# Pre-LN decoder layer on one Trainium2 core: where the causal mask of the self layer's second half of heads is applied

## The reference, cut to what matters

```
x: (16, 128, 128)   16 images (batch entries) of 128 rows (positions) by 128 columns; 16 heads of 8 columns
def self_attention(x):                      # no weights: q = k = v = the heads of x
    w = einsum('bhqd,bhkd->bhqk', q, k) / sqrt(8)
    w = where(tril(ones(128, 128)), w, most_negative)
    return einsum('bhqk,bhkd->bhqd', softmax(w), v)
x = x + self_attention(layernorm(x))
x = x + cross_attention(layernorm(x), ctx, bias)     # projections, bias (16, 16, 128, 128), softmax
x = x + ffn_block(layernorm(x))                      # attention with weights, then 8 experts, one chosen for each row
```

## Time and profile before

| | |
|---|---|
| time, median of 3 runs | 429.36 us (429.25, 429.36, 431.63) |
| span of the profiled execution | 431.3 us |
| time of the profiled execution | not listed apart; 431.63, the slowest of the three, is the only one longer than the span, by 0.3 us |
| busy in the span | PE 313.1, PE weight load 203.1, DVE 249.6, ACT 198.4, POOL 254.1 us |
| self layer (slots 0 to 15) | about 16 to 105 us of the span |
| cross layer with its hand-over from the self layer | about 91 to 212 us |

### The profile page before, as it was taken

The page is one execution under the profiler, slowest core; times in us unless marked ns, Lnnn a source line. Parts: engine busy times, 40 slices in busy tenths (PEclk is TensorE's granted clock), DMA queues, the critical chain, the costliest instruction groups (busy, mean ns, idle before and its releaser), DMA issues.

```text
span 431.3 us, 9910 instructions
## 1 busy us (share of the span) xinstructions
PE 313.1 (73%) x3435; PEld 203.1 (47%) x3435; DVE 249.6 (58%) x592; ACT 198.4 (46%) x390; POOL 254.1 (59%) x365
## 2 busy tenths in 40 slices
PE   1376888776779999989778788898875500199994
PEld 0133333432456666666544444444443400099893
DVE  5135454458999999997356455665622250067773
ACT  3347555544455565565344536456464200045451
POOL 5853343315889898999996638736340327324454
PEclk9969888999999999999899989999997555589998
DMA  6101443210358977921125990000000002323330
GB/s 165 31 2 56 123 117 110 74 38 14 97 156 184 219 191 162 212 27 22 12 26 136 283 297 24 2 2 2 2 2 2 1 24 108 95 53 103 93 90 18
DMA packets 67040, 36.36 MB, mean 84 GB/s; under 512 B 36253, under 2 KB 56864, under 8 KB 66992
## 3 DMA queue, kind: packets, MB, share of 16 engines
q1 hardware_dynamic: 57040, 15.79, 17.4%
q10 hardware_dynamic: 8448, 16.78, 13.7%
q0 software_dynamic: 1504, 3.16, 2.1%
HBM read 28.48 MB, written 7.69 MB: 84 GB/s over the span
## 4 chain that ended last, share of the span: by engine, by line
PE 43%; issue 16%; POOL 15%; DVE 13%; ACT 8%; DVEq 1%; DMA 1%; POOLq 0%; ACTq 0%; SPq 0%
PE pair_banks L562 23%; PE work_bank L562 9%; POOL biased L413 4%; DVE biased L1019 4%; ACT xn L847 4%; POOL routed_rows L545 3%; PE pair_banks L565 3%; PE work_bank L565 3%; PE small_bank L565 3%; PE small_bank L562 2%; POOL rstd L380 2%; DVE rowmax L1034 1%; ACT outT L886 1%; DVE att L1065 1%; POOL q_lane L390 1%
## 5 line engine op out<-in xcount | busy, mean ns | idle before, releaser
L880 ACT ACTIVATE probs<-pair_banks 128x1024 f32<-128x1024 f32 x96 | 97.5, 1023 | 68.6 <-PE pair_banks L565 36.0
L413 POOL TENSOR_TENSOR biased<-biased,rowmax 128x1024 f32<-128x1024 f32 x32 | 60.5, 1899 | 15.7 <-DVE rowmax L1026 15.5
L562 PE MATMUL work_bank<-probs,vaug 128*32 128x128 f32 x1536 | 53.6, 282 | 5.5 <-ACT hn2T L894 3.4
L562 PEld LDWEIGHTS work_bank<-probs,vaug 128*32 128x32 f32 x1536 | 40.3, 112 | 15.7 <-issue 8.6
L1041 DVE TENSOR_TENSOR pair_banks<-pair_banks,causal 128x1024 f32<-128x1024 f32 x16 | 19.7, 1233 | 47.7 <-PE pair_banks L562 47.7
L1034 DVE TENSOR_REDUCE rowmax<-pair_banks 128x8 f32<-128x1024 f32 x32 | 38.9, 1215 | 13.5 <-PE pair_banks L562 13.5
L374 POOL TENSOR_SCALAR vareps<-meanvar 128x2 f32<-128x2 f32 x32 | 7.4, 233 | 62.6 <-DVE meanvar L995 61.5
L562 PE MATMUL pair_banks<-q_lane,kT 32*128 32x512 f32 x256 | 42.3, 734 | 1.7 <-DVE biased L1019 1.7
L1019 DVE TENSOR_TENSOR biased<-pair_banks,bias_in 128x1024 f32<-128x1024 f32 x32 | 38.8, 1214 | 7.3 <-PE pair_banks L562 3.8
L552 POOL DMA_INDIRECT out<-vaug x23 | 22.6, 984 | 33.1 <-DVE vaug L1230 20.3
L562 PE MATMUL pair_banks<-k_lane,qT 32*128 32x512 f32 x256 | 37.5, 654 | 5.9 <-DVE biased L1019 4.0
(11 more groups left out here) (143 smaller groups left out, 581.0 us busy)
## 6 DMA issues: line engine op xcount, KB each, us to landing
bias_in<-in_w SPq DMA_DIRECT2D x16, 256.0 KB, 7.3
routed_rows<-filler SPq DMA_DIRECT2D x2, 1028.0 KB, 9.1
vaug<-routed_rows SPq DMA_DIRECT2D x23, 64.5 KB
biased<-routed_rows SPq DMA_DIRECT2D x23, 64.0 KB
ctx_in<-in_ctx SPq DMA_DIRECT2D x8, 128.0 KB, 4.1
att_scratch<-att SPq DMA_DIRECT2D x16, 64.0 KB, 5.4
att_rows<-att_scratch SPq DMA_DIRECT2D x16, 64.0 KB, 2.9
routed_rows<-filler SPq DMA_DIRECT2D x1, 899.5 KB, 12.0
```

What stands on the lines that cost most here:

```text
L413: nc.gpsimd.tensor_tensor(v, v, rowmax[:, b % 2, 8 * half:8 * half + 8].unsqueeze(2).to_broadcast([128, 8, S]), ALU.subtract).then_inc(s_s ...
L562: return nc.tensor.matmul(o, lhsT, rhs, start=start, stop=stop, **kw)
L880: nc.scalar.activation(probs[:, b % 2, 2 * half:2 * half + 2, :], pair("exp", b, half), ACT.Exp, scale=1.0 if layer(b) == CROSS else SCALE ...
```

## The change

For heads 8 to 15 of the self layer the scores are exponentiated as they are; POOL then multiplies the two quarters `probs[:, b % 2, 2:4, :]` in place by `allowed`, a 128x128 tile of ones and zeros broadcast over the eight heads. `s_masked` now stands for that product, and `add_outputs(b)` waits for it. DVE's addition of the mask is gone, and `exponentials(b, 1)` waits for the scores alone. `allowed` is built by POOL at the start (a memset and a select), in the place of `zero`, which nothing used. The first half is masked as before.

```diff
--- before.py
+++ after.py
@@ -118,7 +118,7 @@
         identb = sb("identb", [128, 128], bf16)
         causal = sb("causal", [128, G, S], bf16)
         pick = sb("pick", [128, G, S], bf16)
-        zero = sb("zero", [128, 1])
+        allowed = sb("allowed", [128, S])
         minus_half = sb("minus_half", [128, 4])
         att_rows = sb("att_rows", [128, 2, D])
         wx = {k: sb("w_" + k, [128, D]) for k in ("xq", "xk", "xv", "xo", "fq", "fk", "fv", "fo")}
@@ -209,6 +209,7 @@
         s_maxT = sem("maxT_ready")
         s_e = sem("scores_ready")
         s_masked = sem("second_half_masked")
+        s_allowed = sem("allowed_ready")
         s_p = sem("probs_ready")
         s_pv = sem("outputs_added")
         s_out = sem("out_copied")
@@ -413,6 +414,13 @@
                 nc.gpsimd.tensor_tensor(v, v, rowmax[:, b % 2, 8 * half:8 * half + 8].unsqueeze(2).to_broadcast([128, 8, S]),
                                         ALU.subtract).then_inc(s_sub, 1)
 
+            def mask_probabilities(b):
+                pool.wait_ge(s_allowed, 2)
+                pool.wait_ge(s_p, 2 * b + 2)
+                v = probs[:, b % 2, 2:4, :].rearrange("p g (h k) -> p (g h) k", k=S)
+                nc.gpsimd.tensor_tensor(v, v, allowed[:].unsqueeze(1).to_broadcast([128, 2 * G, S]),
+                                        ALU.mult).then_inc(s_masked, 1)
+
             def max_parts(b):
                 i, n = b % 2, b - FIRST_FFN
                 pool.wait_ge(s_mfree, 2 * (b - B) + 2)
@@ -474,6 +482,10 @@
             nc.gpsimd.affine_select(out=causal[:], in_=causal[:], compare_op=ALU.is_ge, fill=MASKED, base=0,
                                     pattern=[[0, G], [1, S]], channel_multiplier=-1).then_inc(s_ident, 1)
             inverse_deviation(1)
+            nc.gpsimd.memset(allowed[:], 1.0).then_inc(s_allowed, 1)
+            pool.wait_ge(s_allowed, 1)
+            nc.gpsimd.affine_select(out=allowed[:], in_=allowed[:], compare_op=ALU.is_ge, fill=0.0, base=0,
+                                    pattern=[[1, S]], channel_multiplier=-1).then_inc(s_allowed, 1)
             pool.wait_ge(s_lane, 4)
             self_queries(0)
             pool.wait_ge(s_dve_const, 1)
@@ -512,6 +524,8 @@
                     inverse_deviation(3)
                 if b in LAST_NORMS:
                     inverse_deviation(NP + LAST_NORMS[b])
+                if 1 <= b <= FIRST_CROSS:
+                    mask_probabilities(b - 1)
                 if maxes:
                     subtract_maxes(b + 2, 0)
                 if b % 2 == 0 and CROSS_PAIR <= q + 2 < NP:
@@ -690,6 +704,7 @@
                 claim("work")
                 pe.wait_ge(s_p, 2 * b + 2)
                 if layer(b) == SELF:
+                    pe.wait_ge(s_masked, b + 1)
                     pe.wait_ge(s_vself, b // 2 + 1)
                 else:
                     pe.wait_ge(s_v, b // 2 - CROSS_PAIR + 1)
@@ -872,10 +887,7 @@
                 last.then_inc(s_qkT, 1)
 
             def exponentials(b, half):
-                if layer(b) == SELF and half == 1:
-                    act.wait_ge(s_masked, b + 1)
-                else:
-                    act.wait_ge(s_e, 2 * b + half + 1)
+                act.wait_ge(s_e, 2 * b + half + 1)
                 wait(act, s_pv, b - 1)
                 nc.scalar.activation(probs[:, b % 2, 2 * half:2 * half + 2, :], pair("exp", b, half), ACT.Exp,
                                      scale=1.0 if layer(b) == CROSS else SCALE).then_inc(s_p, 1)
@@ -1034,13 +1046,6 @@
                     nc.vector.tensor_reduce(peak, banks.rearrange("p g (h k) -> p (g h) k", k=S),
                                             AX.X, ALU.max).then_inc(s_mfree, 1)
 
-            def mask_second_half(b):
-                dve.wait_ge(s_ident, 5)
-                dve.wait_ge(s_e, 2 * b + 2)
-                banks = pair("exp", b, 1)
-                nc.vector.tensor_tensor(banks, banks, causal[:].rearrange("p g k -> p (g k)").unsqueeze(1).to_broadcast(
-                    [128, 2, G * S]), ALU.add).then_inc(s_masked, 1)
-
             def take_maxT(b):
                 dve.wait_ge(s_mtr, b - FIRST_FFN + 1)
                 if b - 2 >= FIRST_FFN:
@@ -1102,8 +1107,6 @@
                     norm_stats(NP + LAST_NORMS[b])
                 if maxes:
                     row_maxes(b + 2, 0, FIRST_STEP)
-                if b < FIRST_CROSS:
-                    mask_second_half(b)
                 if 0 <= b - 2 < NB:
                     attention(b - 2)
                 if b == 4:
```

## The result

| | before | changed |
|---|---|---|
| median | 429.31 us (428.9 to 431.63, 4 runs) | 438.92 us (438.42 to 439.2, 4 runs) |
| ratio | | 1.0184, 95% interval 1.0136 to 1.0232 |

The change makes the kernel slower by 1.8%. I had said 430.0 us, range 426.5 to 434.0, and 0.77 for a move within 1%: the time lies outside the range.

A forecast was written before the change was run, and what follows sets the result against it. A chain of waits was taken to bound the self layer. Terms 1.4 - 1.2 - 0.6 + 0.55 = +0.15 us, plus 0.5 for the clock, gave +0.65 on the median 429.36: 430.0 us, range 426.5 to 434.0.

The forecast's parts named there:

- What bounds the kernel, and the chain: Self layer: no engine full, a chain of waits across odd and even slots sets the pace, 9.98 us a pair.
- Even images free, odd ones not: Self layer: even images' products fit 4.5 us before PE wants them; odd images' stand behind the deviation and delay PE.
- The price of one product, 1.90 us: POOL: each of 16 products takes 1.90 us, like the subtraction in place, 30.4 us in all.
- The handover from POOL to PE, 0.05 us: Odd image's chain: 0.05 us between the end of POOL's product and PE's output product.
- the 0.69 that I had: Self layer: the odd image's chain takes 7.28 us against 6.59, so each pair comes 0.69 us later.
- The clock, "0.25 us off" a pair, and 0.5 us once: PE: slow stretch falling partly on a wait saves 0.25 us a pair; longer gaps add 0.5 us once.
- My lag of 1.4 us behind the four pairs: Slot 10: four pairs at 0.45 us each, less 0.4 gained in slot 2, leave 1.4 us of lag.
- Handed back in slots 11 to 13, 1.2 us, and in 14 and 15, 0.6: Slots 11 to 13 each gain about 0.4 us; slots 14 and 15 gain 0.6 from two masks off DVE.
- Hand-over, 0.55 us: Where the cross layer begins: image 14's product fits POOL's idle time, image 15's makes POOL 0.55 us late.
- POOL becomes the bound at the hand-over: Rival, chance 0.12: products of images 14 and 15 cost 1.90 us each in the row-maxima ring; +5.2, 434.6 us.
- The port, priced at 0: DVE's additions to x_sb beside POOL's products cost 0, other end 1.35 us a pair; rival 435.4 us, chance 0.06.
- The gain from removing DVE's mask, 0.37 us in each even slot: Even self slots: the second exponential starts at 50.37 in place of 50.74, gaining 0.37 us if nothing else waits.

The follow-up runs named there:

- e4: Changed kernel with POOL multiplying for images 0, 2, ... 12 only and DVE masking the others: 426.47 us, ratio 0.9882 to before.
- e10: Changed kernel with POOL multiplying for images 1, 3, ... 13 only and DVE masking the others: 437.78 us, ratio 1.0134 to before.
- e9: Changed kernel with seven idle matmuls ahead of PE's wait for each odd image's product (images 3 to 15): 434.60 us, ratio 1.0043 to before.
- e15: Kernel before with five idle matmuls in each even self slot, where PE waits for ACT: 426.37 us, ratio 0.9876 to before.
- e12: Changed kernel without the products of images 14 and 15, nothing in their place: 434.39 us, ratio 1.0057 to before.
- e5: Kernel before, DVE masks kept, with 16 added POOL products on a tile nobody reads and PE not waiting: 435.18 us, ratio 1.0107 to before.
- e8: Changed kernel with DVE's residual addition in the self layer replaced by a reduction with one SBUF input: 434.89 us, ratio 1.008 to before.
- e1: Changed kernel without POOL's product and PE's wait for it, so no mask on heads 8 to 15: 420.90 us, ratio 0.9723 to before.

## Why the prediction was wrong

- **What bounds the kernel, and the chain:** right. The chain through statistics, deviation and product exists as laid out; up to the end of POOL's shift I had 3.73 us and it measures 3.79 (57.64 to 61.43). Even images free, odd ones not: e4 against e10 shows it, 11 us apart.
- **The price of one product, 1.90 us:** wrong, 2.36. I took the subtraction for the same form. It reads a maximum broadcast along its innermost dimension; `allowed` is a full row of 128 values for each head. The operation is not the reason: L390 multiplies, with a mask broadcast along the innermost dimension, and takes 1.89. The Trainium skill, "GPSIMD Engine Reference", section "3.1 Elementwise — side-by-side cycle accounting", lists 4497 ns for an f32 tensor_tensor of 2048 elements with two inputs, thus an estimate of 2.25 us for 1024; the 2.36 here agrees with it within 5%, and would have given the larger price.
- **The handover from POOL to PE, 0.05 us:** it measures 0.24. With the length, that makes 0.65 us a pair more than the 0.69 that I had, so 1.3. Measured at the full clock it is 1.2 (9.64 in e9 against 8.46 in e15).
- **The clock, "0.25 us off" a pair, and 0.5 us once:** wrong, in its sign. Before, PE's wait ends at the transposes, and one slow stretch costs it 1.5 us (9.98 against 8.46). In the changed kernel the slow clock can take in the output product as well as the transposes and the scores, and then costs 2.6 us (12.25 against 9.64). My lag of 1.4 us behind the four pairs measures 5.86 at slot 11. The lag grows there by 6.4 us: 4.7 are length (1.2 a pair, where I had 0.69) and the remaining 1.7 are left for the clock, where I had taken 1.0 off and added 0.5 at the end. The gain ahead of them, 0.4 us, was right (0.51 at slot 3).
- **Handed back in slots 11 to 13, 1.2 us, and in 14 and 15, 0.6:** about right, 1.17 (5.86 to 4.69 at slot 14) and 0.88 (to 3.81 at slot 15).
- **Hand-over, 0.55 us:** the step that failed worst: 3.4 in the trace and 5.0 by e12. I checked that the product of image 14 fits into POOL's idle time ahead of the next *subtraction*, which it does; but PE waits for the product itself, and in POOL's queue it stood behind the subtraction of slot 14. The rival "POOL becomes the bound at the hand-over" (0.12) comes nearest to this, with 434.6 us; it put the wait in the row maxima.
- **The port, priced at 0:** in the self layer right, as far as e5 tells (there, as in the changed kernel, an addition in an even slot takes up to 2.3 us with nothing behind it), at the hand-over wrong: the trace of e8 gives 1.9 us there, the run 4.0 in all. I had also read "1.65 once"; before has a second long addition, 1.22 us at 119.16.
- **The gain from removing DVE's mask, 0.37 us in each even slot:** as a chain about right (a pair at full clock takes 7.98 us in e1, 8.46 in e15), in time far too small: 12 us by e1. Of the 5.9 us that its trace gains between slots 5 and 11, 4.5 are slow stretches that the shorter wait no longer brings (as much as e15 gains there) and 1.4 are length; the rest of the 12 was not taken apart.
- **The execution behind the trace of before**, taken as 431.63: it was one of about 433.1, as said above. The forecast started from the median and does not depend on it.

The terms overlap: what e9, e12 and e8 give back (5.6, 5.0 and 4.0 us) is more than the 7.4 us lost. They can't be added: before gains 5.3 us by idle matmuls too, and the port was met there twice.

## What to carry to other kernels

Ask of an added instruction first which *product* waits for it and what stands ahead of it in its own queue, not whether its engine has idle time; then count, for each lengthened wait of TensorE, on the work behind it at half clock. It does not come each time: here it came behind a wait of 2.92 us and not behind one of 2.27. Take an elementwise POOL instruction's length from a row with the same operand forms, and where one operand is a mask, use a select: 1.10 us against 2.36 here turned a loss of 1.8% into a gain of 2.3%. A split by which images have slack (even ones on POOL) does nearly as well.

## What the runs showed that I had not expected

A POOL tensor_tensor on 128x1024 f32 takes 1.90 us with one operand broadcast along the innermost dimension, 2.36 with that operand a full row, and the select with one input 1.10. Five dead matmuls a pair make the kernel before 5.3 us faster (e15), so 5.3 of the 431 us were the price, in clock, of a wait that itself stays where it is. The same remedy leaves the changed kernel as far behind as it was (7.2 of 7.4 us): a slow clock that one sees in a kernel's trace need not be what a change to it costs.
